# Attention on one Trainium2 core: two heads on two 64-row groups of the array, two PSUM banks per maximum and per exponential, division in query-major form

## The reference

```
def _attn(q, k, v, mask):                         # 16 heads of 8 columns
    scores = einsum('bqhd,bkhd->bhqk', q, k) / sqrt(8)
    scores = where(mask, -inf, scores)
    w = softmax(scores, axis=-1)
    return einsum('bhqk,bkhd->bqhd', w, v)
xn = adaln(x, cond, n1);  q, k, v = split(xn @ qkv.T);  q, k = rope(q), rope(k)
x = x + _attn(q, k, v, src_mask) @ so.T           # self attention, 512 keys
xn = adaln(x, cond, n2);  q = rope(xn @ cq.T);  k = rope(context @ ck.T);  v = context @ cv.T
x = x + _attn(q, k, v, ctx_mask) @ co.T           # cross attention, 77 keys
x = x + feed_forward(adaln(x, cond, n3))
```

## Time and profile before

| | |
|---|---|
| median of 3 executions | 3308.78 us (3301.66 to 3314.81) |
| profiled execution, first to last instruction | 3302.9 us, 46016 instructions |
| its own device time | given only as this span |
| six layers, one of them | 576 to 1007 us of the span |
| in it: projections, maxima ahead, self loop, cross, feed-forward and next start | 27, 19, 229, 107, 49 us |

### The profile page before, as it was taken

One profiled execution on the slowest core, in us unless ns is written; L12 is line 12 of the kernel. 1 busy time (PEld: TensorE's weight loads), 2 busy tenths in 40 slices (PEclk: granted clock), 3 DMA queues, 4 the chain that ended last, 5 costly groups with the idle time before them and its releaser, 6 DMA issues. The chain is left out here.

```text
span 3302.9 us, 46016 instructions
## 1 busy us (share of the span) xinstructions
PE 2654.6 (80%) x16130; PEld 1339.4 (41%) x16130; DVE 2269.1 (69%) x5926; ACT 1611.3 (49%) x2927; POOL 643.8 (19%) x770
## 2 busy tenths in 40 slices
PE   2443996999887998879988799987999878998812
PEld 1322765334452334533345434355343443344511
DVE  7775114888647886478865688655888648886598
ACT  1221332566543665526664366652566534665413
POOL 6110000212212122121221212211222112122124
PEclk9666998899997999979999889998899998999955
DMA  1000000420104111041110231111320103212000
GB/s 37 0 0 26 1 26 8 135 52 31 51 7 137 33 38 43 27 133 31 36 50 22 79 85 42 31 41 37 108 51 30 51 27 117 46 27 61 7 19 13
DMA packets 137617, 148.10 MB, mean 45 GB/s; under 512 B 29527, under 2 KB 119827, under 8 KB 136595
## 3 DMA queue, kind: packets, MB, share of 16 engines
q1 hardware_dynamic: 137375, 144.99, 16.1%
HBM read 81.83 MB, written 60.51 MB: 43 GB/s over the span
## 5 line engine op out<-in xcount | busy, mean ns | idle before, releaser
L1436 DVE TENSOR_REDUCE maxima<-ps 128x1 f32<-128x512 f32 x1536 | 975.9, 680 | 190.1 <-PE ps L908 185.3
L1287 ACT ACTIVATE big<-ps 128x512 f32<-128x512 f32 x1536 | 839.9, 604 | 420.0 <-PE ps L934 417.8
L908 PE MATMUL ps<-k,q 97*128 97x512 bf16 x1536 | 626.4, 410 | 19.3 <-DVE maxima L1436 10.4
L934 PE MATMUL ps<-q,k 128*128 128x512 bf16 x1536 | 591.6, 389 | 0.0
L945 PE MATMUL ps<-big,vaug 128*32 128x512 f32 x3072 | 411.8, 608 | 1.4 <-ACT big L1287 1.4
L934 PEld LDWEIGHTS ps<-q,k 128*128 128x128 bf16 x1536 | 151.8, 99 | 344.7 <-ACT big L1287 206.2
L908 PEld LDWEIGHTS ps<-k,q 97*128 97x128 bf16 x1536 | 152.7, 100 | 223.0 <-DVE maxima L1436 118.4
L1377 POOL COPY big<-invsum 128x512 f32<-128x512 f32 x90 | 55.0, 611 | 960.8 <-DVE invsum L1454 960.8
L1508 DVE TENSOR_REDUCE maxima<-ps 128x4 f32<-128x308 f32 x384 | 167.5, 472 | 73.0 <-PE ps L1030 70.4
L1321 ACT ACTIVATE hat<-ps 128x512 f32<-128x512 f32 x192 | 112.9, 602 | 131.8 <-PE ps L1049 131.5
L1384 POOL TENSOR_TENSOR big<-big 128x512 f32<-128x512 f32 x48 | 55.2, 1156 | 622.4 <-ACT big L1259 619.0
(11 more groups left out here) (311 smaller groups left out, 4332.3 us busy)
## 6 DMA issues: line engine op xcount, KB each, us to landing
q<-scratch_queries SPq DMA_DIRECT2D x36, 768.0 KB, 5.7
k<-scratch_keys SPq DMA_DIRECT2D x36, 384.0 KB, 8.3
scratch_queries<-big SPq DMA_DIRECT2D x30, 384.0 KB, 2.4
w<-in_w SPq DMA_DIRECT2D x6, 1600.0 KB, 7.2
scratch_keys<-big SPq DMA_DIRECT2D x24, 384.0 KB, 4.6
scratch_queries<-big SPq DMA_DIRECT2D x30, 256.0 KB, 2.7
scratch_queries<-xnT SPq DMA_DIRECT2D x18, 384.0 KB, 2.4
scratch_keys<-big SPq DMA_DIRECT2D x24, 256.0 KB, 4.7
```

The costliest lines, as they stand in the source:

```text
L908: nc.tensor.matmul(m.ps[:, s_bank + at % 3, :], m.q6[0:ROWS_MAX, b % 2, 2 * g + h // 2, qt * P:(qt + 1) * P], m.k6[0:ROWS_MAX, b % 2, 4 * ...
L934: nc.tensor.matmul(m.ps[:, st_bank + at % 3, :], m.k6[:, b % 2, 4 * g + j, kt * P:(kt + 1) * P], m.q6[:, b % 2, 2 * g + j // 2, :], start= ...
L1287: nc.scalar.activation(m.probs[:, at // 4 % 2, at % 4, :], m.ps[:, st_bank + at % 3, :], ACT.Exp, scale=scale).then_inc(probs, 1)
L1436: nc.vector.reduce_max(m.maxima[:, qt, h:h + 1], m.ps[:, s_bank + at % 3, :], AX.X).then_inc(s_read, 1)
```

## The change

`q6`, `k6` and `kc6` hold a pair of heads on rows 0 to 51 and 64 to 115: each head has its own 48 product rows, its mask row and three shift rows, and there are no zero rows. `k6` shrinks to one column block per pair. The scores of a pair are two matmuls on two row groups into two neighbouring banks. One DVE reduction then yields the maxima of both heads, one ACT instruction both exponentials. Banks 0 to 5 are three double banks, handed round to maxima, exponentials and cross maxima alike in the order in which the program issues them. The maxima run 14 pairs ahead. The unit is transposed once, DVE takes the reciprocal of the sums and multiplies in query-major form (16 heads x 8 columns for four tiles); once per batch these rows are transposed back (`turn_on`), copied by ACT (`copy_on`) and projected by one matmul per tile, with unpadded weights. `spread_inverse` and POOL's `widen` are gone. The cross attention goes through the same slots as units 16 to 31; its queries have tiles of their own (`cq3` and a part of `big`).

```diff
-ROWS_HEAD = HD * PRODUCTS
-ROW_MASK = 2 * ROWS_HEAD
+ROW_BLOCK = P // 2
+ROW_MASK = HD * PRODUCTS
 ROW_SHIFT = ROW_MASK + 1
 ROWS_MAX = ROW_SHIFT
-ROWS_ALL = ROW_SHIFT + 6
+ROWS_ALL = ROW_SHIFT + 3
...
+    per_unit, lead, late = 2 * TB, 14, 16
+    selfs, crosses, c_items = UNITS * per_unit, B * PAIRS, B * TB * 2
+    turn_from = (B - 1) * PAIRS
+    def exp_at(p):
+        return 2 * p + (late if p >= selfs + turn_from else 0)
+    def pv_at(quad):
+        return exp_at(2 * quad + 1) + 5
+    def done_at(u):
+        return pv_at(TB * u + TB - 1 if u < UNITS else TB * UNITS + u - UNITS)
+    def gather_at(u):
+        return done_at(u) + (6 if u < UNITS else 4)
+    def divide_at(u):
+        return gather_at(u) + 1
+    def turn_on_at(j):
+        return divide_at(GROUPS * j + GROUPS - 1) + 1
+    def cmax_at(i):
+        first, step = ((229, 2), (245, 2), (269, 2), (turn_on_at(2 * B - 2) + 4, 0))[i // (2 * TB)]
+        return first + i % (2 * TB) * step
...
+    project_of = {turn_on_at(j) + 4: j for j in range(2 * B)}
+    steps = 2 * per_unit
+    c_turn_of = {249: 0, 265: 1, 286: 2, turn_on_at(2 * B - 2) + 4: 3}
+    r_add_at, r_turn_at, r_product_at = turn_on_at(B - 1) + 4, 273, (277, 281)
+    order = [("max", i) for i in range(lead)]
+    for at in range(end):
+        order += [("exp", exp_of[at])] if at in exp_of else []
+        order += [("max", max_at(at))] if max_at(at) is not None else []
+        order += [("cmax", i) for i in cmax_of[at]]
+    slot = {item: k for k, item in enumerate(order)}
+    def banks(kind, i):
+        first = 2 * (slot[kind, i] % 3)
+        return m.ps[:, first:first + 2, :]
...
+            def free_banks(kind, i):
+                k = slot[kind, i]
+                if k >= 3:
+                    before, j = order[k - 3]
+                    pe.wait_ge({"max": s_read, "exp": probs, "cmax": c_s_read}[before], j + 1)
+                return banks(kind, i)
+            def max_scores(i):
...
+                out = free_banks("max", i)
+                for u in range(2):
+                    rows = slice(u * ROW_BLOCK, u * ROW_BLOCK + ROWS_MAX)
+                    last = nc.tensor.matmul(out[:, u], m.q6[rows, b % 2, 2 * g + pr, qt * P:(qt + 1) * P], m.k6[rows, b % 2, 2 * g + pr, :],
+                                            start=True, stop=True)
+                last.then_inc(s_ready, 1)
...
+            for at in range(end):
+                n, s = at // steps, at % steps
+                if at in exp_of:
+                    shifted_scores(exp_of[at])
+                if max_at(at) is not None:
+                    max_scores(max_at(at))
+                if at in pv_of:
+                    weigh_values(pv_of[at])
+                for i in cmax_of[at]:
+                    c_max_scores(i)
+                if s == 7 and n + 1 < UNITS:
                     turn_maxima(n + 1)
+                if at in project_of:
+                    project_out(project_of[at])
+                if at in turn_on_of:
+                    turn_on(turn_on_of[at])
+                if at in gather_of:
+                    gather_sums(gather_of[at])
...
+                if n % 4 == 2 and 2 < n < UNITS and s == 9:
                     turn_state(n // 4)
+                if n % 4 == 2 and n < UNITS and s == 13:
+                    product(n // 4, 0)
+                if n % 4 == 3 and n < UNITS and s == 1:
+                    product(n // 4, 1)
...
+                nc.vector.tensor_reduce(m.smax[:, qt, :, pr], banks("max", i), AX.X, ALU.max).then_inc(s_read, 1)
...
+            def divide_unit(u):
+                dve.wait_ge(sums_ready, u + 1)
+                turned = m.ps[:, aux, :].rearrange("p (t h r) -> p t h r", t=TB, h=4)
+                nc.vector.reciprocal(m.invsum[:], turned[:, :, :, HD]).then_inc(inverted, 1)
+                dve.wait_ge(inverted, u + 1)
+                nc.vector.tensor_tensor(m.on_rows[:, :, 4 * g:4 * g + 4, :], turned[:, :, :, 0:HD],
+                                        m.invsum[:].unsqueeze(3).to_broadcast([P, TB, 4, HD]), ALU.mult).then_inc(on, 1)
...
             def load_pairs(b, i0, i1, loaded):
-                src = a["queries"][b].rearrange("(i r) c n -> (r c) i n", i=PAIRS)
-                sp.dma_start(m.q6[0:ROW_MASK, b % 2, i0:i1], src[:, i0:i1]).then_inc(loaded, 16)
                 for u in range(2):
+                    lo = u * ROW_BLOCK
+                    src = a["queries"][b].rearrange("(i u r) c n -> u (r c) i n", u=2, r=HD)
+                    sp.dma_start(m.q6[lo:lo + ROW_MASK, b % 2, i0:i1], src[u][:, i0:i1]).then_inc(loaded, 16)
...
```

More of the change, by code:

```diff
@@ new lines, in attend, with max_at @@
+    copy_of = {copy_at(u): u for u in range(units)}
+    gather_of = {gather_at(u): u for u in range(units)}
+    divide_of = {divide_at(u): u for u in range(units)}
+    turn_on_of = {turn_on_at(j): j for j in range(2 * B)}
+    project_of = {turn_on_at(j) + 4: j for j in range(2 * B)}
+    end = turn_on_at(2 * B - 1) + 5
+    steps = 2 * per_unit
+    total = UNITS * steps
+    def max_at(at):
+        i = at // 2 + lead
+        return i if at % 2 and at < total and i < selfs else None
+    cmax_of = {at: [i for i in range(c_items) if cmax_at(i) == at] for at in range(end)}
@@ new lines, in shifted_scores @@
+                out = free_banks("exp", p)
+                for u in range(2):
+                    rows = slice(u * ROW_BLOCK, u * ROW_BLOCK + ROWS_ALL)
+                    if p < selfs:
+                        keys, queries = m.k6[rows, b % 2, 2 * g + pr, kt * P:(kt + 1) * P], m.q6[rows, b % 2, 2 * g + pr, :]
+                    else:
+                        keys, queries = m.kc6[rows, b, pair, :], m.cq[b][rows, pair, :]
+                    last = nc.tensor.matmul(out[:, u], keys, queries, start=True, stop=True)
@@ new lines, in shifted_scores @@
+                last.then_inc(st_ready, 1)
+            def weigh_values(quad):
+                if quad < selfs // 2:
+                    n, kt = quad // TB, quad % TB
+                    b, g = n // GROUPS, n % GROUPS
+                    first, final, values = kt == 0, kt == TB - 1, m.vaug[:, b, kt]
+                else:
+                    n = UNITS + quad - selfs // 2
+                    b, g = n // GROUPS - B, n % GROUPS
+                    first, final, values = True, True, m.vcaug[:, b]
+                pe.wait_ge(probs, 2 * (quad + 1))
+                if first and n >= 1:
@@ L976, in context_values, with project_out @@
+                last.then_inc(on_ps, 1)
+            def project_out(j):
+                pe.wait_ge(on_sb, j + 1)
+                take_aux(added, j + 1)
+                for t in range(TB):
+                    last = nc.tensor.matmul(m.ps[:, aux, t * P:(t + 1) * P], m.on[:, t * P:(t + 1) * P], w_of(m, "so" if j < B else "co"),
+                                            start=True, stop=True)
+                last.then_inc(o_ps, 1)
             def context_values():
@@ new lines, in product, with c_max_scores @@
+                nc.tensor.matmul(m.ps[:, aux, 0:n], w_of(m, name), rhs, start=True, stop=True).then_inc(x_ps, 1)
+            def c_max_scores(i):
+                b, qt, half = i // (2 * TB), i % (2 * TB) // 2, i % 2
+                if i == 0:
+                    pe.wait_ge(x_stacked, 16 * 2 * B)
+                if i % (2 * TB) == 0:
+                    pe.wait_ge(c_kq[b], 32 if b < B - 1 else 64)
+                out = free_banks("cmax", i)
+                for pair in range(PAIRS // 2 * half, PAIRS // 2 * (half + 1)):
+                    for u in range(2):
+                        rows, lo = slice(u * ROW_BLOCK, u * ROW_BLOCK + ROWS_MAX), pair % (PAIRS // 2) * N_CTX
+                        last = nc.tensor.matmul(out[:, u, lo:lo + N_CTX], m.cq[b][rows, pair, qt * P:(qt + 1) * P],
+                                                m.kc6[rows, b, pair, 0:N_CTX], start=True, stop=True)
@@ L1106, in _ @@
                     turn_normal(B - 1)
-                banks = product_banks[i % 2]
+                two = product_banks[i % 2]
                 if i >= 2:
```

771 lines of the change are left out of this document (261 added, 510 removed).

## The result

The changed kernel takes 3202.14 us (median of 4 runs, 3194.78 to 3203.74), the one before 3307.95 beside it: a ratio of 0.967, 95% interval 0.966 to 0.969. Forecast were 3150 us, likeliest between 3060 and 3240. The profiled execution took 3194.78 us and spans 3193.1, 109.8 less than before, where 158 were forecast.

The account below looks back on a forecast made before the run. PE was taken to bound the self loop, latency cross attention. Per layer +1 (lead) - 9 (loop) - 17 (cross) = -25, six times -150, setup -8: span 3145, time 3150 us; likeliest 3060 to 3240, range 2990 to 3320.

Parts of the forecast that it names:

- The ring: Self loop: value group, exp's scores, exp on ACT, maximum's scores waiting for its banks, next value group; 2.95 us per group.
- The self loop: Self attention per layer: 62 value-group periods, 183 us, plus extras and short waits; 220 us against 229.
- The statistics: Self loop: DVE's eleven small operations fall together with the splitting of maxima in three units; 3 x 1.5, 4.5 us.
- The row groups: Score matmuls: two heads on separate rows overlap, second starting 0.05 us later; frees 3.3 of 14.3 us per unit.
- Rival 2: Score matmuls: row groups run one after the other; loop 240, cross 96, no change at 3308 us; chance 0.12.
- Cross attention: Cross stage per layer: value groups, products, pause before batch 3 and tail; 90 us against 107, bounds 80 and 102.
- Due 9 slots later, free: Extra DMAs in SP's queue: same bytes, due over 6 us later, so free; else 1-2 us a unit.
- The changes of tiling: PE: each transpose, product and projection adds two tiling changes, 0.25 us each; about 4 us a layer on the path.
- The setup term: Setup: POOL's fills end about 12 us earlier, so DVE stands still less; -8 us, bounds 0 and -15.
- DVE as the bound (1): Self loop: exps start or groups end earlier, so DVE bounds it; loop 191, cross 85, total 2947 us; chance 0.15.
- Bursts on top of the ring (3): Shared buffers: DVE bursts stall all three engines; loop 240 to 245, cross 98, total 3300 to 3330 us; chance 0.12.
- The clock (4): Self loop: PE's clock stays at 1.2 GHz, 4.4 us per value group, +90 us a layer, 3690 us; chance 0.11.

Follow-up runs that it names:

- pv4: Changed kernel with the value group issued one item earlier, behind the odd exp's scores instead of the maximum's: 3345.3 us, 1.011 of before.
- half_max: Changed kernel with each self-attention maximum reading only the first 256 of 512 keys: 3181.8 us, 0.9635 of before.
- first_close: Changed kernel with batch 0's eight cross maxima issued two by two at items 229 to 235, not singly at 229 to 243: 3163.3 us, 0.957 of before.
- same_rows: Changed kernel with both heads of every score pair on the first 64 rows, so nothing overlaps: 3969 and 4008 us in the two fastest of four runs.
- early_max: Changed kernel with the last batch's cross maxima at items 299 to 306, turned at 309, before batch 2's output projection: 3193.9 us, 0.967 of before.
- compact: Changed kernel with the last round's products and splits closer, last maxima at 291 to 298, empty items 4 instead of 16: 3221.6 us, 0.975 of before.
- turn_later: Changed kernel with the last batch's state transposes at item 277, products at 280 and 282, batch 2's cross maxima at 277 to 284: 3222.3 us, 0.974.
- twice: Changed kernel with each cross exp's pair of score matmuls issued twice into its banks: 3197.6 us, 0.9675 of before.
- close_early: Changed kernel with the edits of first_close and early_max together: 3164.7 us, 0.957 of before.
- split: Changed kernel with exps in the self loop on double bank 0 and maxima on 1 and 2: 3254.0 us, 0.985 of before.

## Why the prediction was right, and where not

**The ring: right.** 2.95 us forecast, 2.83 at the shortest. The 0.12 between them is the second head, counted with 0.07 ahead of the exp and 0.05 in the maximum's pair, where it costs nothing; the other terms (1.00, 0.43, 1.03, 0.06, 0.22 and about 0.09 for the change of tiling) came out as forecast. It was shown twice: the value group's place alone changes which engine closes it (`pv4`), and 60 us of DVE work do not matter (`half_max`). DVE is busy 87% of the first 228 items, forecast 85%; the maximum takes 1.22 us, the exp 1.03, as forecast 1.19 and 1.03.

**The self loop: right, 220 forecast, 217 measured.** By units of the third layer, from the start of one's exp scores to the next one's, 215 us in all; what a unit takes beyond 11.88, the length of one without extras, is put down to what it has:

| | forecast | measured |
|---|---|---|
| rings and maxima transposes | 190.5 | 16 units at 11.88: 190 |
| turning rows and projection, 3 times | 5.7 | 2.4 + 1.9 + 1.8 |
| state transposes and products | 5 + 3 | 3 x 2.1 |
| statistics | 4.5 | 0: the three units that have them take 11.88 |
| splitting of maxima beside GpSimd (and in two of the three units a product) | in the 4.5 | 0.7 + 2 x 1.45 |
| start and clock, first two units | 7 | 3.9 |
| last unit (cross maxima beside it) | 0 | 5.2 |

The last row is what the forecast lacks: it gave the last 28 items 20 to 22 us, and they took 28 to 29.5. It counted the cross maxima as work beside the ring, and they share its banks. At a clock of 0.69 to 0.80 some of it is the clock; 2 to 3 us go away in `first_close`, with the hole beside GpSimd and with a better clock.

That 217 came so near 220 is in part luck. The ring was forecast 0.12 too long, 7 us over 62 rings, and 4 us were kept for short waits; that paid for the last unit and for the rest that lies beside the rings.

The statistics were forecast to hurt and did not. The fourth, eighth and twelfth unit have what the last one has beside the cross maxima: DVE's splitting of the loop's own maxima stands still beside GpSimd's rotation.
```profile
712.37 1.26 POOL L1280 TENSOR_TENSOR hat<-hat,cos 128x512 f32<-128x512 f32 x1 [12.32 <-ACT hat L1170]
712.47 1.19 DVE L1332 TENSOR_TENSOR smax<-smax,mparts 128x16 f32<-128x16 f32 x1
...
713.69 1.21 DVE L1333 CAST mparts<-smax 128x16 bf16<-128x16 f32 x1
```
Elsewhere these two take 0.18 us. In `half_max`, where they come ahead of the rotation and take 0.18, the three units are 0.7, 0.7 and 1.15 us shorter. No run moves them alone, so this cause is likely and not shown, and what moving them would give is open.

**The row groups: more than forecast.** 3 ns instead of 0.05 us. The Trainium skill, "TensorE: Matmul & The Clock Gate", section "Why this matters for your kernels", says that matmuls on distinct row groups start within 4 ns; the trace agrees. With it the ring is shorter by the 0.12 above, not by 0.05, and the loop by 7 us a layer, not 3. (The pairs free 2.7 us of PE's time per unit by the prediction's own 0.22 and 0.27, not its 3.3; nothing in the sum rests on it.) Rival 2 is dead for this kernel, but `same_rows` shows what it would have been without overlap: 25 us a layer, more than the whole gain, before the clock is counted. No run puts back the old division and projection, so what their removal gave is not measured.

**Cross attention: the step that was mis-sized, 90 forecast, 101 to 109 measured,** outside the bounds of 80 to 102 in two layers, and just outside in a third (102.6). In the first layer: batches 0 to 2, forecast 51, took 60.5; emptying and pause, forecast 16.6, took 19.2; batch 3 and tail, forecast 19.5, took 21.4.
- "Due 9 slots later, free" was wrong of the shift rows. Batch 2's maxima are turned at item 286, its first exp is at 288. In the trace PE waits 2.52 us there for the DMA, and ACT 3.40.
- The clock was put at 1.5 us for the pause alone. The stage got 0.81, before 0.97. A value group takes 1.93 us at the low clock, where the fast one takes 1.07; the first batch alone differs by 7.3 us between layers, and two of six had the slow one.

Five edits there (`early_max`, `compact`, `turn_later`, `twice`, and `close_early` over `first_close`) gained nothing that can be measured, or lost. The wait that an edit was aimed at went or shrank; as much came back as a wait behind it, or in the clock. Why batch 1 takes 27.5 us when its known waits (statistics 4.3, divisions 1.7, the scaling 1.0) are taken off is not settled.

**The changes of tiling.** The prediction put them at 4 us a layer. The one ahead of a value group takes about 0.1 us, as before the change (696.28 to 696.60, less 0.22); no run measures the others.

**The sum.** Forecast -25 a layer and -8: -158. Measured: 14 more per layer in cross attention (mean 104), 4 less in the loop, 1.5 less after it: 6 x 8.5 = 51 us short of it; in fact 48 are missing. (The mean of 104 is 93.7 us from first to last cross exp over the six layers, and 10.3 around it as in the first.) The span accounts for 48 of the 52 us between 3150 and 3202; the rest is that the median lies 9 us above the profiled span here, where 5.9 were put on top. The setup term was right: DVE's statistics of `x` begin at 37.86 us instead of 45.73.

**The rivals.** DVE as the bound (1) is answered by `half_max`. Bursts on top of the ring (3) are there, but small: the mean period is 0.44 above the shortest, with PE's own extras in it, and `half_max` took 0.08 of that; `split` did not bring the mean down. The clock (4), given 0.11, did not happen in this kernel's loop (0.95), but it is near: `same_rows` has it, with groups 5.8 to 6.8 us apart where I had worked out 4.4 for pairs that overlap, and in cross attention a part of it did happen.

## What to carry over

When several readers share buffers on an in-order engine, write down who stands behind the long instruction and which reader it waits for: that ring, not any engine's share, was the loop's length, and one item of order moved it by 29 us a layer. In a stage bound by latency the sum of its work says little: follow each wait in the queue, and each transfer issued shortly ahead of its use. And look for small operations that take 1.2 us where others of their kind take 0.2: moving four of them a layer went with 39 us here (34 by the ratios to the kernel before), nearly half of it where they stood and the rest with the clock of the next batch, while reordering the rest of the stage gained nothing.

## What the hardware showed

- DVE's small copies and subtractions between SBUF tiles stand still beside GpSimd's 128x512 operations (0.2 us becomes 0.82 to 1.27, in all six layers, and 0.18 becomes 1.19 to 1.21 in the loop), while a reduction out of PSUM doesn't: in `first_close` the one at 822.28 takes 0.80 us beside the rotation at 822.33, and 0.795 is the mean of the 32 in the changed kernel's first layer. The Trainium skill, "SBUF — State Buffer", section "Who interferes with whom", says that on VectorE copies and casts can contend with GpSimd for a shared pair of ports, that an operation with two SBUF inputs contends with a GpSimd instruction that reads SBUF, and that a reduction never contends on this chip. The trace agrees, in all three kinds of operation.
- In `same_rows` the granted clock fell to 0.50 in a loop in which the records show PE busy all the time (50.00 of 50 us) and the array did two matmuls one after the other that it had done side by side. What the engine's busy time says is no guide to it.
- The same stretch of the same program, the first cross batch of `compact`, takes 16.9, 21.2 or 24.0 us from layer to layer, at a mean clock of 1.00, 0.72 and 0.54. An edit's effect of under 7 us a layer can be hidden or made by that, so it has to be read from the stretch and not from the total.
